# Segment sums from differences of running sums in one fp32r pass, and two projection products moved earlier, in a fused Mamba and mixture-of-experts layer

## The reference, cut to what matters

```python
A = -jnp.exp(A_log)
def step(h, inp):
    x_t, dt_t, B_t, C_t = inp
    dA = jnp.exp(dt_t * A)
    h = h * dA[:, :, None, None] + (dt_t[:, :, None] * x_t)[..., None] * B_t[:, None, None, :]
    y = jnp.einsum('bhpn,bn->bhp', h, C_t)
    return (h, y)
```

## Time and profile before

| | us |
|---|---|
| median of 3 runs | 859.13 |
| lowest and highest | 858.85, 860.33 |
| profiled execution, its time | 856.96 |
| profiled execution, its span | 855.1 |
| TensorE busy in the span | 784.8 (92%) |
| VectorE busy | 617.1 (72%) |
| ScalarE busy | 498.4 (58%) |
| GpSimd busy | 321.3 (38%) |
| mean granted TensorE clock | 0.992 of full |

### The profile page before, as it was taken

The page is one execution under the profiler, slowest core; times in us unless marked ns, Lnnn a source line. Parts: engine busy times, 40 slices in busy tenths (PEclk is TensorE's granted clock), DMA queues, the critical chain, the costliest instruction groups (busy, mean ns, idle before and its releaser), DMA issues. The chain is left out here.

```text
span 855.1 us, 18101 instructions
## 1 busy us (share of the span) xinstructions
PE 784.8 (92%) x5472; PEld 481.4 (56%) x5472; DVE 617.1 (72%) x1469; ACT 498.4 (58%) x928; POOL 321.3 (38%) x600
## 2 busy tenths in 40 slices
PE   2779999999999989999899999999899998999997
PEld 1554564755547555665647555475556656474645
DVE  2686569685887858787696857878587876978634
ACT  2425784476753776557844667537764577446652
POOL 5423624054521716037250545217260372505400
PEclk9998999999999999999999999999999999999999
DMA  4000000000000100000000000000000000000000
GB/s 167 1 3 20 14 1 2 9 16 26 0 2 14 30 0 0 8 13 25 0 0 8 14 25 0 1 6 28 11 0 8 13 26 0 0 8 14 25 2 13
DMA packets 15145, 11.73 MB, mean 14 GB/s; under 512 B 1040, under 2 KB 13968, under 8 KB 14992
## 3 DMA queue, kind: packets, MB, share of 16 engines
q1 hardware_dynamic: 15120, 11.43, 4.4%
HBM read 7.76 MB, written 2.10 MB: 12 GB/s over the span
## 5 line engine op out<-in xcount | busy, mean ns | idle before, releaser
L1102 ACT ACTIVATE sb_pr<-S 128x768 f32<-128x768 f32 (+1 forms) x192 | 161.2, 878 | 130.0 <-PE S L445 129.4
L1198 DVE TENSOR_REDUCE sb_mx<-S 128x2 f32<-128x256 f32 (+3 forms) x256 | 198.1, 818 | 33.2 <-PE S L445 32.0
L1722 POOL TENSOR_SCALAR_AFFINE_SELECT sb_pr<-sb_pr 128x256 f32<-128x256 f32 (+1 forms) x192 | 98.1, 517 | 298.2 <-ACT sb_pr L1102 297.7
L445 PE MATMUL R<-sb_pr,sb_va 128*32 128x512 f32 (+3 forms) x1024 | 89.7, 445 | 6.2 <-ACT sb_pr L1102 3.4
L445 PE MATMUL R<-sb_W,sb_pr 128*128 128x96 f32 (+1 forms) x512 | 69.5, 276 | 0.0
L445 PE MATMUL R<-sb_xfT,sb_W 128*128 128x512 f32 x144 | 69.2, 602 | 0.0
L445 PE MATMUL S<-sb_kT,sb_qT 32*128 32x256 f32 (+3 forms) x512 | 56.3, 384 | 13.2 <-DVE sb_mx L1198 9.3
L445 PEld LDWEIGHTS R<-sb_W,sb_pr 128*128 128x128 f32 x512 | 63.5, 192 | 3.8 <-issue 3.5
L445 PEld LDWEIGHTS S<-sb_kT,sb_qT 32*128 32x128 f32 x512 | 27.5, 183 | 65.9 <-DVE sb_mx L1198 58.0
L1432 DVE SCALAR_TENSOR_TENSOR sb_x<-R,sb_wts,sb_x 128x96 f32<-128x96 f32 x128 | 40.6, 317 | 22.8 <-PE R L445 19.4
L445 PE MATMUL S<-sb_qT,sb_kT 32*128 32x256 f32 (+3 forms) x512 | 56.3, 384 | 0.5 <-ACT sb_pr L1102 0.5
(11 more groups left out here) (217 smaller groups left out, 1719.0 us busy)
## 6 DMA issues: line engine op xcount, KB each, us to landing
sb_xin<-x SPq DMA_DIRECT2D x9, 256.0 KB, 2.8
sb_W<-weights SPq DMA_DIRECT2D x1, 2290.0 KB, 10.4
sb_qT<-sb_mT SPq DMA_DIRECT2D x128, 4.0 KB
sb_xres<-x SPq DMA_DIRECT2D x8, 256.0 KB, 2.8
out<-sb_xres SPq DMA_DIRECT2D x7, 256.0 KB, 2.3
sb_cT<-sb_xact SPq DMA_DIRECT2D x8, 128.0 KB, 2.3
sb_W<-weights SPq DMA_DIRECT2D x1, 514.0 KB, 5.1
sb_cst<-consts SPq DMA_DIRECT2D x1, 328.0 KB, 3.0
```

Source lines behind the costliest of these rows:

```text
L445: return pe.matmul(o, lhsT, rhs, start=start, stop=stop, skip_group_check=True)
L1102: act.activation(pr[:, e % 4, :, 0:n], S[pair_of_exp(e)][:, :, 0:n], ACT.Exp).then_inc(p_sb, 1)
L1198: o = dve.tensor_reduce(mx[:, n // P - 1, g, heads[0]:heads[1] + 1], found[:, :, at_col:at_col + n], AX.X, ALU.max, negate=True)
L1722: pool.affine_select(out=keep, in_=keep, compare_op=ALU.is_ge, fill=0.0, base=0, pattern=pattern, channel_multiplier=-1)\
```

## The change

- The segment sum over s < k <= t is now written as the difference of two running sums. VectorE takes the running sums out of S[0] in two parts, a rounded fp32r part and the rest (`sums_in_parts`, two instructions), into `cs`. TensorE transposes `cs` (`turn_sums`, into R[1]). ScalarE makes from it `seg_v` (one activation) and `seg_l` (four, one per chunk), all 128 x 128 with a per-partition scale and bias. GpSimd spreads `seg_v` over the heads once, `seg_r` (128 x 512). `segments(c)` is then a single fp32r product of `seg_l[:, c]` and `seg_r`.
- GpSimd's four `decays` of a round are gone; the one `seg_r` product takes their place at the start.
- Differences with s > t are positive, so `es` can be large there; VectorE's product of `es` and `gm` takes the smaller of `es` and 1 first.
- Ahead of `segments` of chunk 0, `dense(R[1], 2)` runs: two fp32 products of 256 columns.
- `experts_down(3)`, which writes R[1], waits for `seg_l`.
- `h2a` gets a buffer of its own.
- The `qkv` product of token block 0 moves from stage b to the end of stage a, ahead of `turn_y(3)`; that of block 1 moves ahead of the eight `op` products.
- At the start of the program VectorE makes the small selection tables (6 reductions), ahead of its other set-up, and GpSimd clears `cs`.

```diff
+            def turn_sums(r):
+                pe.wait_ge(cs_sb, at(cs_sb, r, 2))
+                pe.wait_ge(act_up, at(act_up, r, 17))
+                pe.transpose(R[1][:, 0:P], cs[:].rearrange("p c k -> p (c k)"), ident).then_inc(csT_ps, 1)
+
             def segments(r, c):
-                pe.wait_ge(rs_sb, at(rs_sb, r, c + 1))
+                if c == 0:
+                    pe.wait_ge(moe_sb, at(moe_sb, r, 4 * E))
+                    pe.wait_ge(segl_sb, at(segl_sb, r, 1 + T))
+                    dense(R[1][:, 0:256], 2)
+                pe.wait_ge(segl_sb, at(segl_sb, r, 1 + T))
+                pe.wait_ge(segr_sb, at(segr_sb, r, 1))
...
-                mm(R[1][:, :], after, rs[:, c % 2].rearrange("p h t -> p (h t)")).then_inc(seg_ps, 1)
+                mm(R[1][:, :], seg_l[:, c, :], seg_r[:].rearrange("p h t -> p (h t)")).then_inc(seg_ps, 1)
...
+                if t == 3 and head:
+                    pe.wait_ge(segl_sb, at(segl_sb, r, 1 + T))
...
+                if head:
+                    project_qkv(r, 1)
+                if tail:
 
                     pe.wait_ge(yT_sb, at(yT_sb, r, 0))
...
-                    for t in range(T):
-                        mm(bank(t)[:, 0:3 * D], xbT[:, t * P:(t + 1) * P], w("qkv")).then_inc(qkv_ps, 1)
+                    for t in range(2, T):
+                        project_qkv(r, t)
...
                 weigh_values(r, G * UNITS - 2)
+                pe.wait_ge(xbT_sb, at(xbT_sb, r, 1))
+                pe.wait_ge(p_sb, at(p_sb, r, G * UNITS))
+                project_qkv(r, 0)
                 turn_y(r, T - 1)
...
+                    if e == 0:
+                        act.wait_ge(csT_ps, at(csT_ps, r, 1))
+                        act.wait_ge(segr_sb, at(segr_sb, r, 0))
+                        act.activation(seg_v[:], R[1][:, 0:P], ACT.Identity, bias=seg_sums[:, 1:2],
+                                       scale=seg_sums[:, 0:1]).then_inc(segl_sb, 1)
+                        act.wait_ge(seg_ps, at(seg_ps, r, 0))
+                        for c in range(T):
+                            act.activation(seg_l[:, c, :], R[1][:, 0:P], ACT.Identity, bias=seg_low[:, c:c + 1],
+                                           scale=seg_high[:, c:c + 1]).then_inc(segl_sb, 1)
...
+            def sums_in_parts(r):
+
+                total = S[0][:, 0, 0:T * NH].rearrange("p (c h) -> p c h", h=NH).unsqueeze(2)\
+                    .broadcast_to([P, T, 2, NH])
+                parts = cs[:, :, 0:16].rearrange("p c (x y h) -> p c x y h", x=2, y=2)
+                dve.wait_ge(dec_sb, at(dec_sb, r, 1))
+                dve.wait_ge(csT_ps, at(csT_ps, r, 0))
+                dve.tensor_copy(parts[:, :, :, 0].bitcast(F32R), total).then_inc(cs_sb, 1)
+                dve.wait_ge(cs_sb, at(cs_sb, r, 1))
+                tt(parts[:, :, :, 1], total, parts[:, :, :, 0], ALU.subtract).then_inc(cs_sb, 1)
...
-                tt(wm[:, c % 2], es[:, c % 2], gm[:, c % 2, :].unsqueeze(1).broadcast_to([P, NH, P]),
-                   ALU.mult).then_inc(wm_sb, 1)
+                stt(out=wm[:, c % 2], in0=es[:, c % 2], scalar=1.0,
+                    in1=gm[:, c % 2, :].unsqueeze(1).broadcast_to([P, NH, P]),
+                    op0=ALU.min, op1=ALU.mult).then_inc(wm_sb, 1)
...
-            def decays(r, c, tail):
-
-                pool.wait_ge(dt_sb, at(dt_sb, r, DT_STEPS))
-                if c == 0 and tail:
-                    pool.wait_ge(up_ps, at(up_ps, r, 9))
-                pool.wait_ge(seg_ps, at(seg_ps, r, c - 1))
-                tt(rs[:, c % 2], upto.unsqueeze(1).broadcast_to([P, NH, P]),
-                   dta[:, c, :].unsqueeze(2).broadcast_to([P, NH, P]), ALU.mult).then_inc(rs_sb, 1)
-
             def stage_a(r, tail):
-                decays(r, 0, tail)
+                pool.wait_ge(segl_sb, at(segl_sb, r, 1))
+                pool.sem_inc(pool_passed, 1)
+                pool.wait_ge(seg_ps, at(seg_ps, r, 0))
+                tt(seg_r[:], seg_v[:].unsqueeze(1).broadcast_to([P, NH, P]),
+                   seg_head[:].unsqueeze(2).broadcast_to([P, NH, P]), ALU.mult).then_inc(segr_sb, 1)
...
-                    if u == 5 and g < T - 1:
-                        decays(r, g + 1, tail)
```

More of the change, by code:

```diff
@@ L178, in build @@
         dec = sb("dec", [P, 3, T, NH])
-        rs = sb("rs", [P, 2, NH, P])
         es = sb("es", [P, 2, NH, P])
+        cs = sb("cs", [P, T, 32])
+        seg_v = sb("seg_v", [P, P])
+        seg_l = sb("seg_l", [P, T, P], F32R)
+        seg_r = sb("seg_r", [P, NH, P], F32R)
+        seg_low = sb("seg_low", [P, T])
+        seg_high = sb("seg_high", [P, T])
+        seg_sums = sb("seg_sums", [P, 2])
+        seg_head = sb("seg_head", [P, NH])
         gm = sb("gm", [P, 2, P])
@@ L215, in build @@
         h1 = sb("h1", [P, 2, L])
+        h2a = sb("h2a", [P, 2, L])
         h3a = sb("h3a", [P, L])
@@ L273, in build @@
         cum_ps = signal("cum_ps", 1)
+        csT_ps = signal("csT_ps", 1)
         seg_ps = signal("seg_ps", T)
@@ L690, in project_z, with project_qkv @@
                 mm(bank(t)[:, 0:DI + NH], xaT[:, t * P:(t + 1) * P], w("zdt")).then_inc(z_ps, 1)
+            def project_qkv(r, t):
+                mm(bank(t)[:, 0:3 * D], xbT[:, t * P:(t + 1) * P], w("qkv")).then_inc(qkv_ps, 1)
             def dense(o, n):
@@ L842, in stage_b @@
                 if head:
+                    turn_sums(r)
                     exp_scores(r, 0)
@@ L900, in _ @@
             pe.wait_ge(c_loaded, 48)
-            pe.wait_ge(pool_set, 10)
-            pe.wait_ge(dve_set, 7)
+            pe.wait_ge(pool_set, 11)
+            pe.wait_ge(dve_set, 13)
             pe.wait_ge(xab_sb, at(xab_sb, -2, 1))
@@ L905, in _ @@
             pe.wait_ge(wh_loaded, 16)
+            pe.wait_ge(xbT_sb, at(xbT_sb, -1, 0))
+            project_qkv(-1, 0)
             stage_b(-1, False, True)
@@ L1422, in stage_b @@
                        ALU.add).then_inc(sv_sb, 1)
+                if head:
+                    sums_in_parts(r)
                 for t in range(T):
@@ L1552, in _ @@
             dve.tensor_copy(maskb[:], future).then_inc(dve_set, 1)
+            by_part = ident.rearrange("p (c k) -> p c k", c=T)
+            dve.tensor_reduce(seg_low[:], by_part[:, :, 0:8], AX.X, ALU.add).then_inc(dve_set, 1)
+            dve.tensor_reduce(seg_high[:], by_part[:, :, 8:16], AX.X, ALU.add, negate=True).then_inc(dve_set, 1)
+            dve.wait_ge(dve_set, 4)
+            dve.tensor_reduce(seg_sums[:, 0:1], seg_low[:], AX.X, ALU.add).then_inc(dve_set, 1)
+            dve.tensor_reduce(seg_sums[:, 1:2], seg_high[:], AX.X, ALU.add, negate=True).then_inc(dve_set, 1)
+            dve.tensor_reduce(sp[:, 0], by_part[:, :, 0:16].rearrange("p c (m h) -> p c h m", h=NH),
+                              AX.X, ALU.add).then_inc(dve_set, 1)
+            dve.wait_ge(dve_set, 7)
+            dve.tensor_reduce(seg_head[:], sp[:, 0].rearrange("p c h -> p h c"), AX.X,
+                              ALU.add).then_inc(dve_set, 1)
             ts(wqk[:], row[:, R_QN:R_QN + HD].unsqueeze(1).broadcast_to([P, AH, HD]), HD ** -0.5, None,
                ALU.mult).then_inc(dve_set, 1)
-            dve.wait_ge(dve_set, 3)
+            dve.wait_ge(dve_set, 9)
             tt(wqk[:], wqk[:], row[:, R_KN:R_KN + HD].unsqueeze(1).broadcast_to([P, AH, HD]),
```

13 lines of the change are left out of this document (7 added, 6 removed).

## The result

The changed kernel took 847.88 us (median of 4 runs, 847.36 to 848.38) against 858.99 for the kernel before on the same chip (4 runs, 857.32 to 860.33): ratio 0.987, 95% interval 0.984 to 0.990. The forecast was 852.1 with a range of 848.5 to 857.0. On the two profiled executions it was 8.7 us (span 855.1 to 846.4).

What follows compares the result with a forecast made beforehand. TensorE is 92% busy, but exponentials, masks and GpSimd's queue were taken to bound the edited places. Seven loop rounds at -1.35 give -9.45, prologue and ends +2.45: net -7.0, from 859.13 to 852.1 us, range 848.5 to 857.0.

Steps and rivals of the forecast that it cites:

- Group 3: Chunk 3's product with values waits 1.12 us for GpSimd's masks; without decays ahead in the queue, gain 0.95 a round.
- Boundary: End of stage a into stage b: two qkv products moved earlier bring the squares forward, gain 0.6 us a round.
- Chunk 0: Two fillers plus the pass take 1.25 us in place of 1.10 behind the expert outputs; cost 0.2 a round.
- groups 1 and 2: Chunks 1 and 2: exponentials and masks replace the shortened product as the wait; gain 0.1 in the first, 0 in the second.
- The fp32r pass: Price of the new single segment product on TensorE, taken as 0.25 us, between 0.16 and 0.56.
- The prologue: Stage a there has no expert products to cover the new operands' set-up; cost 2.2 us, between 1 and 4.
- the set-up: Prologue's preparation of new operands: five ScalarE activations ahead of the exponential of e = 1 delay TensorE's scores by 2.0 us.
- 1: All TensorE time counts at every product the change touches: 25 us gained, 834 us; chance 0.04.
- 2: GpSimd's freed time at chunk 3's masks is not passed on: 858.8 us; chance 0.10.
- 3: Moving the qkv products gives nothing, since the delayed output projection becomes late: 856.3 us; chance 0.13.
- 4: GpSimd's power for the norms locks VectorE out at chunk 2's yz, cutting chunk 3's gain to 0.6: 854.6 us; chance 0.07.
- Rival 5: New idle time in chunks 1 to 3 makes TensorE's clock fall once every round: slower, 876.6 us; chance 0.04.

Runs made afterwards that it cites:

- e4: Changed kernel with the segment products of chunks 1 to 3 as plain fp32, two recorded matmuls each; 848.20 us.
- e2: Changed kernel with three unused 128x512 products put on GpSimd where the kernel before had its decays; 864.57 us.
- e6: Kernel before with only GpSimd's order changed, decays of chunks 2 and 3 one group earlier; 851.06 us.
- e3: Changed kernel with all four query, key and value products back in stage b, behind the output projection; 851.62 us.
- e7: Kernel before with the decays earlier on GpSimd and query, key and value products 0 and 1 moved as in the change; 847.06 us.
- e12: Changed kernel with filler products in stage b of the loop and in the prologue; 844.22 us.
- e11: Kernel before with decays earlier, two query products moved, and fillers in stage b of the loop and in the prologue; 842.41 us, ratio 0.979.
- e9: Kernel before with three filler products in the waits of the loop's stage b; 857.01 us, ratio 0.9965.
- e1: Changed kernel measured again with no edit; 848.99 us.
- e10: Kernel before, no edit, run for a second profile; 859.8 us.
- e5: Changed kernel without the two filler products ahead of the segment pass of chunk 0; 854.41 us.
- e8: Changed kernel with three filler products in the waits of the loop's stage b; 846.13 us.

## Why the forecast of faster was right, and its size wrong

**What bounds.** Right. TensorE is busy 92% and three passes shortened by 0.6 us each are worth 0.13 a round (e4), where 1.8 would be the naive count. The unused idle time shows up in front of the scores, released by the exponentials and not, as predicted, by the mask; of the whole kernel, before and after:

```profile
L445 PE MATMUL S<-sb_qT,sb_kT 32*128 32x256 f32 (+3 forms) x512 | 56.3, 384 | 0.5 <-ACT sb_pr L1102 0.5
L455 PE MATMUL S<-sb_qT,sb_kT 32*128 32x256 f32 (+3 forms) x512 | 56.5, 385 | 7.6 <-ACT sb_pr L1136 7.6
```

**Group 3.** Right, mechanism and size: 0.98 for a forecast of 0.95, undone by GpSimd work alone (e2, +0.96) and obtained by GpSimd's order alone (e6, -0.97). It is the largest term, and it has nothing to do with the pass itself.

**Boundary.** Right: 0.65 for 0.6 (e3, e7). The delayed output projection stayed hidden: nothing between the squares and the next `dec` moved by it.

**Chunk 0, groups 1 and 2.** Chunk 0 +0.17 for +0.2; group 1 -0.15 for -0.1; group 2 within 0.05 of nothing. The transpose's +0.1 was taken up by the row maximum that the next scores wait for, so stage a of the loop gained 0.88 where the terms said 0.75. With the boundary that makes 1.3 us over seven rounds.

**The fp32r pass.** Taken at 0.25, measured 0.47 to 0.50, and 0.58 behind the fillers. It moved the time little: even 0.6 more in groups 1 to 3 is worth 0.13 a round (e4), and chunk 0 cost no more than forecast.

**The prologue.** This is the step that failed: "I take +2.2, between 1 and 4", together +2.45 with the ends of the program; measured -1.0. The 3.4 between them has four parts.

The first is the set-up, 1.25 too large. In stage a of the prologue it costs 0.95 with the clock full in both kernels (e12 against e11). The prediction let the exponential of e = 1 hold back the whole stage by 2.0. The scores of e = 2 did wait for it:

```profile
67.87 0.44 PE L455 MATMUL S<-sb_qT,sb_kT 32*128 32x384 f32 x2 [0.97 <-ACT sb_pr L1146]
```

That is e12; they come 1.75 later there than in e11. But the next scores, those for the row maxima, stand 0.83 behind them in e11, waiting for VectorE, and start together with them in e12. So one exponential later the delay was 1.17, and at the end of the stage 0.95: the path had slack that the sum left out.

The second is group 3 of the prologue. The prediction found the wait of 1.12 only in the loop and gave the prologue nothing; but a wait of 0.51 stood there, before and after:

```profile
99.56 0.16 PEld L445 LDWEIGHTS R<-sb_pr,sb_va 128*32 128x32 f32 x8 [0.51 <-POOL sb_pr L1722]
98.55 0.17 PEld L455 LDWEIGHTS R<-sb_pr,sb_va 128*32 128x32 f32 x8 [0.38 <-POOL sb_pr L1784]
```

From the start of the exponentials (96.59 and 95.98) to this product it is 2.97 and 2.57: 0.40 gained. 0.95 less 0.40 comes to the +0.54 of the table. GpSimd's clearing, forecast at 0.2, moved the first `xbT` by 0.04, 0.16 less.

The third is chance: the sum treated the half-clock stretches of one execution as fixed. The kernel before had 0.50 to 0.87 from 28 to 34 us, the changed one a full clock there:

```profile
30.00:32.00 2.00, 2.00 (x10) 2.00 (x11) 0.00 (x0) 0.60 (x1) 1.55 (x5) 0.50 0.00 0
30.00:32.00 2.00, 2.00 (x21) 2.00 (x20) 1.19 (x2) 1.36 (x4) 1.78 (x4) 1.00 0.00 0
```

That gave 1.1: `sq` to `dec` is 41.23 and 40.13, and 40.13 in e9 too, the kernel before with a full clock at this place. The second stretch, in stage a, has the same length in both (6.8 us) and by this sum gave nothing. The fourth part, 0.5, is chance as well: the first `qkv` products took 5.46 us before and 4.94 after, though they start no earlier, and in e1, the changed kernel again, 5.46 (in this order):

```profile
16.54 5.46 PE L445 MATMUL S<-sb_W,sb_xbT 128*128 128x384 f32 x8 [1.49 <-issue]
16.62 4.94 PE L455 MATMUL S<-sb_W,sb_xbT 128*128 128x384 f32 x8 [1.54 <-ACT sb_xbT L993]
16.62 5.46 PE L455 MATMUL S<-sb_W,sb_xbT 128*128 128x384 f32 x8 [1.54 <-ACT sb_xbT L993]
```

So 1.6 of the 3.4 is luck. In e1 it went the other way: up to `dec` +1.54, stage a +0.38, together +1.9, which by number is close to the forecast.

**From profile to median.** The sum added 2.2 for the distance of the median from the profiled execution, a distance that it did not explain. It is for the most part falls of the clock in the loop (e10). The profiled execution of before had none; by the 2.2 its median run has one or two (an estimate, at 1.36 each). The profiled one of after had two, which is why the medians differ by 11.1 and the profiles by 8.7. Without loop falls it is 856.96 against 848.16 - 2.7 = 845.5, a gain of 11.5 against 7.0: the prologue's miss is 3.4, the loop's 1.3, and 0.3 was lost again in the first loop round. Less the 1.6 of chance in the prologue, some 9.9 is the change itself. Measured once more, the changed kernel took 848.99, within the range: a part of the miss is this scatter of 1 us.

**The rivals and the signs.** 1, 2, 3 are out (e4; e2 and e6; e3). 4 did not occur: the combination of chunk 2's y under the power kept its durations. Two of the prediction's own signs of being wrong did show: a stretch of lower clock in the loop, and TensorE waiting for the exponential of e = 1 (in the prologue). Rival 5, the clock falling in every round, didn't come true for this change, but falls of the clock are a real mechanism of this kernel: e2 and e5 are slower by it, 9 and 8 us beyond what their undisturbed rounds say, and it had a chance of 0.04. Its "against" was wrong: waits of 0.9 us with a full clock in one trace don't show that they are harmless, since in the next execution (e10) the clock fell behind such a wait.

## What to carry to other kernels

Where an engine is late by one instruction, look first at what stands ahead of it in its own queue: moving GpSimd's products by one group and two products of TensorE gave what the new formulation gave with them, without its set-up. A profile is one execution: before a sum is made on a median, take a second profile and see whether the distance between the two is made of rounds with a lower granted clock. Where such rounds exist, filler products in the waits in front of them can be worth more than the time they take. In the changed kernel they gave 2.9 us in the loop's stage b, where they cost next to nothing (e8 against e1), 4.8 with those of the prologue (e12 against e1), which cost 0.45, and 5.4 at chunk 0 (e5), where they cost 0.32 a round.

## What the chip showed that was not expected

- The granted clock of TensorE fell, always to 0.50 (1.2 GHz), in a loop in which TensorE is 92% busy. In stage b it fell at one step only, behind waits of 0.93, 0.32 and 0.34 us within 5 us, in none to four of the seven rounds of a profile; each fall cost 1.33 to 1.38 us. In stage a it fell only where a wait had been made longer (e2) or fillers left out (e5). The Trainium skill, page "TensorE: Matmul & The Clock Gate", section "A second HAM failure mode: psum-queue depth-cycling", tells of a kernel whose clock goes up and down because the array idles often and briefly between groups; the trace agrees, and e8 shows that filling the idle time ends it.
- Which rounds have a fall changes from execution to execution with no change of code (the third and sixth of the loop's seven in one, the last in the next). The Trainium skill, page "TensorE: Matmul & The Clock Gate", section "What's actually happening", has the activity watched on a count that doesn't start with the kernel, which could make it so; no run here tests that.
- An fp32r product with 128 rows, 128 columns of weights and 512 columns is one recorded matmul of 0.47 to 0.50 us at full clock (0.58 right behind the fillers of chunk 0); the fp32 one is two, 1.02 to 1.12 together. ScalarE's activations of 128 x 128 out of PSUM with bias and scale take 0.45 and follow each other every 0.35.
- VectorE's difference of two tiles in SBUF (`mhl`) took 0.81 to 0.98 beside GpSimd's product, once in each stage a, and 0.18 the other three times. In the changed kernel it takes 0.18 always (mean 177 ns of 32, below). With the unused products of e2 the 0.98 is back, eight times of 32 (mean 377):

```profile
L1251 DVE TENSOR_TENSOR sb_mhl<-sb_mx,sb_mhl 128x16 f32<-128x16 f32 x32 | 5.7, 177 | 1.4 <-DVE sb_mhl L1249 0.3
```
